# From the first attention to the experts: turned blocks copied ahead of gated products, normalised rows copied ahead of exponentials, downs three blocks behind

## The reference, cut to what matters

```
x = x + attention1(layernorm(x))          # 16 heads of 16, causal, with biases
x = x + experts(layernorm(x))             # 4 experts by token id, weights = ctx
x = x + ffn(layernorm(x))                 # second attention (16 heads of 128) and 16 routed experts
experts(h): for e in 0..3:
    z = h @ ctx[e].T                      # Wg and Wu are the same matrix
    y = (silu(z) * z) @ ctx[e].T          # Wd is that matrix too
    out = where(expert_of(token) == e, y, out)
```

## Time and profile before

| | |
|---|---|
| median of 3 timed executions | 678.64 us |
| lowest and highest of them | 677.57 and 681.84 us |
| the profiled execution: its time | 685.46 us |
| the profiled execution: its span | 683.7 us |
| mean granted TensorE clock in it | 0.96 |

### The profile page before, as it was taken

One profiled execution on the slowest core, in us unless ns is written; L12 is line 12 of the kernel. 1 busy time (PEld: TensorE's weight loads), 2 busy tenths in 40 slices (PEclk: granted clock), 3 DMA queues, 4 the chain that ended last, 5 costly groups with the idle time before them and its releaser, 6 DMA issues.

```text
span 683.7 us, 13478 instructions
## 1 busy us (share of the span) xinstructions
PE 625.1 (91%) x4132; PEld 545.1 (80%) x4132; DVE 424.6 (62%) x1134; ACT 350.0 (51%) x1120; POOL 323.9 (47%) x402
## 2 busy tenths in 40 slices
PE   7789888899888999999999999995879899999897
PEld 4667666698777999999999999995768699877774
DVE  4686887477846666666666666664685685444324
ACT  2567877233365756565666565665420155433320
POOL 7888886001634343334333333355201567777740
PEclk9899999799999999999999999997796999999999
DMA  5998910040000201020101020131730433323318
GB/s 168 217 161 190 159 19 1 1 145 1 1 1 1 63 1 61 0 61 0 61 0 61 0 61 0 51 115 40 160 115 9 131 122 102 101 101 104 106 63 307
DMA packets 27985, 52.36 MB, mean 77 GB/s; under 512 B 4235, under 2 KB 16011, under 8 KB 27851
## 3 DMA queue, kind: packets, MB, share of 16 engines
q1 hardware_dynamic: 22371, 38.79, 21.7%
q0 software_dynamic: 4512, 12.33, 5.7%
q10 hardware_dynamic: 1056, 0.66, 0.5%
HBM read 39.31 MB, written 12.45 MB: 76 GB/s over the span
## 4 chain that ended last, share of the span: by engine, by line
PE 61%; DVE 12%; POOL 9%; issue 6%; ACT 6%; DMA 4%; SPq 1%; ACTq 0%; DVEq 0%; POOLq 0%
PE bank L226 40%; PE bank L1660 3%; POOL yb L1472 2%; PE bank L1136 2%; DMA hx<-yb 2%; PE bank L1219 2%; DMA yb<-hx,dst 2%; POOL p L626 2%; PE bank L1587 2%; PE bank L505 1%; PE bank L1127 1%; POOL h L1467 1%; DMA x<-in 1%; PE bank L1619 1%; PE bank L1630 1%
## 5 line engine op out<-in xcount | busy, mean ns | idle before, releaser
L279 POOL TENSOR_TENSOR p_sb<-p_sb,prec 128x256 f32<-128x256 f32 (+1 forms) x128 | 62.2, 507 | 139.1 <-DVE prec L273 139.1
L266 ACT ACTIVATE p_sb<-bank,nmax 128x256 f32<-128x256 f32 x64 | 30.4, 475 | 89.6 <-DVE nmax L259 89.6
L616 ACT ACTIVATE p<-bank,nmax 128x256 f32<-128x256 f32 (+1 forms) x128 | 52.6, 426 | 21.4 <-DVE nmax L608 21.0
L626 POOL TENSOR_TENSOR p<-p,rec 128x512 f32<-128x512 f32 x48 | 50.1, 1054 | 18.5 <-DVE rec L621 18.2
L1472 POOL DMA_INDIRECT yb<-hx,dst x47 | 47.8, 1017 | 20.2 <-issue 11.9
L226 PE MATMUL bank<-hTh,w3h 128*128 128x512 f32 x128 | 53.0, 414 | 1.8 <-DVE hTl L220 1.8
L226 PE MATMUL bank<-G,xTh 128*128 x188 | 51.3, 355 | 0.0
L226 PE MATMUL bank<-hTh,w3l 128*128 128x512 f32 x128 | 50.4, 394 | 0.0
L226 PE MATMUL bank<-hTl,w3h 128*128 128x512 f32 x128 | 50.0, 391 | 0.0
L273 DVE RECIPROCAL prec<-psum_ 128x2 f32<-128x2 f32 x64 | 10.6, 166 | 63.3 <-ACT p_sb L268 63.3
L1660 PE MATMUL bank<-wd,hx 88*128 x188 | 49.2, 385 | 0.0
(11 more groups left out here) (263 smaller groups left out, 2123.3 us busy)
## 6 DMA issues: line engine op xcount, KB each, us to landing
Gf<-in SPq DMA_DIRECT2D x16, 352.0 KB, 5.0
qk<-staged SPq DMA_DIRECT2D x36, 128.0 KB, 6.2
staged<-qk SPq DMA_DIRECT2D x8, 512.0 KB, 9.0
w<-in SPq DMA_DIRECT2D x16, 256.0 KB, 3.4
wd<-in SPq DMA_DIRECT2D x1, 2816.0 KB
wv<-in SPq DMA_DIRECT2D x9, 256.0 KB, 3.6
wo<-in SPq DMA_DIRECT2D x9, 256.0 KB, 2.7
hx<-yb SPq DMA_DIRECT2D x2, 1024.0 KB, 10.2
```

Of the source, the lines that this page charges most:

```text
L266: act.activation(p_sb[:, k, 0:256], S_PS[k][:, 0:256], ACT.Exp, bias=nmax[:, k, 0:1], accum_out=sums[0]).then_inc(u.ex, 1)
L279: pool.tensor_tensor(p, p, r.to_broadcast(p.shape), ALU.mult).then_inc(u.pn, 1)
L616: act.activation(job.probs(n % 2)[:, k, :], job.scores()[:, k, :], ACT.Exp, bias=nmax1[:, n % 2, i:i + 1], accum_out=sums1[:, n % 2, i:i + ...
L626: pool.tensor_tensor(p, p, rec1[:, n % 2, job.stats].unsqueeze(2).to_broadcast(p.shape), ALU.mult)\
```

## The change

- `act_job`: the ScalarE copy of a turned chunk of normalised rows (n = 13 and 15) goes ahead of the JC exponentials of that quad.
- `LAG` goes from 2 to 3: down(v - 3) follows z(v), and three downs are left behind z15. The output product and the transposes keep their rounds (3 and 5), and so do the copies of the second half (round 6) and the residual's place relative to the downs.
- down0 waits for 7 of the attention's 8 chunk copies (`s_oe1`), not for all 8. The eighth empties bank 6, which down0 does not write; `pe_wo1` still waits for it.
- VectorE: the JB copy goes from round 1 to round 0, the JC copy from 2 to 1, `dve_o1` from 3 to 2, `dve_apply2` of sequence 2 from 1 to 3.
- The statistics of the third layernorm keep their rounds (11 and 12) under the new LAG.

```diff
         def act_job(act, k):
             n, job = k // 3, JOBS[k % 3]
+            done = F_JOBS.get(n)
+            if job is JC and done and done[0] == "turn":
+                hT_scalar(act, n2, 0, high=True, chunks=(done[1],))
             if n < NQ:
                 act_exp1(act, n, job)
...
-            elif job is JC and done and done[0] == "turn":
-                hT_scalar(act, n2, 0, high=True, chunks=(done[1],))
...
-        LAG = 2
+        LAG, WO_AT, TURN_AT = 3, 3, 5
...
                 if v == 0:
                     pe.wait_ge(JC.pt, NQ)
-                    pe.wait_ge(s_oe1, 2 * B)
+                    pe.wait_ge(s_oe1, 2 * B - 1)
...
-                if v == LAG + 1:
+                if v == WO_AT:
                     pe_wo1(pe, B - 1)
-                if v == LAG + 3:
+                if v == TURN_AT:
...
-                if v == LAG + 4:
+                if v == TURN_AT + 1:
                     hT_scalar(act, n2, 1, high=True)
...
-                if v == 1:
+                if v == 0:
                     dve_e1(dve, NQ - 1, JB)
+                elif v == 1:
+                    dve_e1(dve, NQ - 1, JC)
+                elif v == 2:
+                    dve_o1(dve, B - 1, 1)
+                elif v == 3:
                     dve_apply2(dve, B - 2)
-                elif v == 2:
-                    dve_e1(dve, NQ - 1, JC)
-                elif v == 3:
-                    dve_o1(dve, B - 1, 1)
...
-                if v == GX + LAG + 1:
+                if v == GX + LAG:
                     dve.wait_ge(s_x2, GT // 2)
-                if v in (GX + LAG + 1, GX + LAG + 2):
-                    first = 2 * (v - GX - LAG - 1)
+                if v in (GX + LAG, GX + LAG + 1):
+                    first = 2 * (v - GX - LAG)
```

More of the change, by code:

```diff
@@ L718, in act_job @@
                 act_e1(act, n - 1, job)
-            done = F_JOBS.get(n)
             if job is JC and done and done[0] == "qk":
```

## The result

The changed kernel takes 673.25 us (median of 11 executions, 670.51 to 676.12). The kernel before, timed beside it, has a median of 680.5 us; the ratio is 0.9904, 95% interval 0.9879 to 0.9930. One of its 11 executions was a slow one, at 711.25 us, and does not count in the ratio. By the ratio the change is worth 6.5 us, give or take 1.7, which is 0.96% and so just short of the 1% to which the forecast gave a chance of 0.67. The forecast was 670.1 us, a ratio of 0.9874, in a range of 667 to 675; 673.25 lies in that range, and outside the forecast case's own 667 to 672. The profiled execution has a span of 673.7 us, where the sum gave 683.7 less 9.8, 673.9.

A forecast was written before the change was run, and what follows sets the result against it. TensorE was taken as the bound, busy for 625.1 of 683.7 us. Of 9.8 us in the profile (1.4 + 8.4), 5.1 of waits and 3.4 of clock reach the median: 678.64 - 8.5 = 670.1 us, range 667 to 675.

The forecast's parts named there:

- forecast case: The main case, full clock from z0 on: 670.1 us, own range 667.0 to 672, chance 0.63.
- the sum: Row-by-row pricing of TensorE's work from z0 to z6 at full clock: 9.8 us off the profiled execution.
- The order laid out by hand: Predicted times from z0 (117.4) to z6 where attention meets experts: TensorE goes on without a stop over 0.5 us.
- the two later stops: TensorE's waits at the residual (1.14 us) and the third layernorm's transposes (1.41 us), claimed to stay.
- Part 1: ScalarE's hTh copy ahead of the JC exponentials: 1.1 us before z0 plus 0.35 at n = 13, say 1.4 us.
- part 2: VectorE's new order and lag 3 in the first expert blocks: 8.4 us, assuming full clock.
- The lag: Downs three blocks behind: down0's factors and banks over 1 us early, where lag 2 came after `dve_o1`.
- the loosened wait: down0 waiting for 7 of 8 chunk copies: costs nothing and saves nothing more.
- The rival in which it falls at the seam all the same: Low clock still granted between attention and experts: gain only 5.1 to 6.8 us, 671.8 to 673.5 us, chance 0.20.
- the Trainium skill's rule on transposes: Transposes do not bring full clock, so z0 could start slow: 8.1 us instead of 9.8.
- From the profiled execution to the median: Step from 9.8 us in the profile to 8.5 in the median: 5.1 of waits, 3.4 of 4.7 low clock.
- What stays: From z6 on, rounds the same with one more down outstanding: 0, with ±0.3 us.

The follow-up runs named there:

- experiment 3: Kernel before with VectorE's new order and down0's loosened wait, downs still two blocks behind, ScalarE's copy as before: ratio 0.9932, 675.75 us.
- experiment 5: Kernel before, order untouched, with 17 matmuls of zeros put into TensorE's stops where the first attention meets the experts: ratio 0.9969, 679.36 us.
- 6: Kernel before, unchanged, profiled twice more: span 678.2 us in the first of the two traces, stage 66.6 and 66.3 us.
- experiment 7: Changed kernel, unchanged, timed and profiled again on a second chip: ratio 0.9888 to the kernel before, 673.37 us.
- Experiment 9: Changed kernel with 8 or 16 matmuls of zeros between its last down and the second attention: 0.9927, 675.4 us and 0.9948, 676.43 us.
- experiment 8: Changed kernel with first residual moved into round 10 and third layernorm's rows one round earlier: 0.9812, 667.76 us; with the residual alone 0.9882, 672.79 us.

## Why the prediction was right, and where it was off

**The stage.** The order laid out by hand held nearly to the row: z0 at 117.29 for 117.4, z2 at 120.95 for 120.9, the value product at 122.51 for 122.3, the transposes at 133.55 for 133.1, no stop before z6, the two later stops unchanged. The span shrank by 10.0 us where the sum had 9.8, which is luck in part: the end of the stage came 9.5 us earlier (185.03 to 175.56), and 0.5 us came from behind it, where the sum had nothing.

**Part 1** was priced at 1.4 us. In the traces it moves z0 by 1.7: 0.5 at n = 13 (the value product of quad 12 to that of quad 14 takes 10.82 us and not 11.35; the sum had 0.35) and 1.2 at n = 15 (the value product to z0 takes 0.79 and not 1.98). Alone it meets a longer wait for the JC copy, and no gain can be measured; on top of part 2 it is worth 3.2 us by the ratios, with an interval of over 2 to either side. In the traces part 1 takes 2.2 to 2.5 us off the stage alone and 2.8 on top of part 2, each time with the low clock over z0 and z1 gone. That the parts help each other is thus suggested by the timed runs only, and not shown.

**The lag** was credited with down0's freedom. The order alone has the same stage (61.7 against 61.9 us) and the lag alone gives nothing measurable (0.9984). With z0 late, as in those kernels, down0's low part was ready 0.1 us ahead; whether the lag is needed once part 1 is in was not tried. The changed kernel's trace speaks against it: low(0) is written from 122.54 for 0.68 us, and z3, which stands where down0 would stand with lag 2, starts at 123.30, so the low part would be ready 0.1 us ahead there too (an estimate from these two rows). What the sum called worth nothing, the loosened wait, is worth something exactly in that case (experiment 3).

**The clock.** The rival in which it falls at the seam all the same did not come about, and the Trainium skill's rule on transposes ("TensorE: Matmul & The Clock Gate", Part 4), by which z0 would start slow, would have given 8.1 us for the profile; the span shrank by 10.0. The stretch from 115.58 to 118.95 has 2.76 us busy, partly with turns, and a clock of 1.00, and z0 starts fast. So the slow start did not come about. Most of the matmuls in that stretch are of other kinds, though (16 of the 27 are the value product's), and whether turns alone would hold the clock no run here shows.

**The step that was off** is "From the profiled execution to the median". I forecast 8.5 us for the median, 5.1 for the waits and 3.4 for the clock; it was 6.5 by the ratio (4.8 to 8.2). The waits were right: 4.8 us in the stage (experiment 5) and 0.5 ahead of it. The clock's share was too large. I took the low time at the seam rightly, 6.8 us in two of three traces of the kernel before, but counted half of it as lost, 3.4, where taking it away was worth 2.4 to 2.7 (experiments 5 and 6), since TensorE at full clock waits longer for VectorE. Against those two traces that makes 5.3 + 2.5 = 7.8 us.

The other 1.3 us down to 6.5 are within the interval; the repeat in experiment 7 has 7.6 (5.0 to 10.2). There is a hint that they are real. "What stays" put the later stages at 0 ± 0.3, but the rest of the program takes 494.3 to 498.9 us with the same instructions, and both traces of the changed kernel lie at the long end. The timed runs of the kernel before have a mean clock of 0.9656, about 47 us at the low level, of which 7 to 10 at the seam; those of the changed one have 0.968, about 43, and none at the seam in any trace. Outside it the low time would have risen by some 3 to 6 us. But the mean clock of the kernel before differs from chip to chip by as much as 3 us of low time (0.9641 to 0.9663), so this is a hint and no more.

**What stays open** is whether the changed seam moves low clock into the later stages at all, and if so why. Experiment 9 can't tell, and two or three traces of each kernel can't tell a habit of an order from chance. The same doubt hangs over the 2.5 us that experiment 8 seems to have gained beyond its stage, and over part 1's missing gain.

## What to carry to other kernels

Where two stages meet, lay out the queue of the engine that hands over, row by row; here moving four short VectorE steps by one or two rounds, with one wait loosened, freed the matrix engine, and more distance between producer and consumer did not. A gap costs twice where the clock falls behind it, so price the low stretches beside the waits, but at less than half their length where the engine then waits for another one anyway, and from several executions: of three profiles of one kernel, one had 3.4 us more low clock at the seam and a rest 4 us longer. Once the seam is tight, look for the next stops of the same kind in the trace; two that stood in plain sight gave 3.1 us of the stage.

## What the runs showed of the hardware

Matmuls of zeros in the idle slots of TensorE, 17 of 0.22 us, kept the granted clock at 1.00 over a seam where it fell twice in three of three traces of the kernel before. A low stretch of 3.4 us ahead of a wait for VectorE delayed TensorE's next step behind that wait by 0.8 us only. Low clock was not confined to visible gaps: the second trace of the changed kernel had 3.4 us of it from 99 to 104 us, inside the first attention, where none of the other traces had any.
